# Layernorm passes moved into the head loop of a differential attention kernel, group by group

## What is computed

```
x = x + layernorm(differential_attention(layernorm(x)))   # 16 heads of 8
x = x + layernorm(windowed_transformer(layernorm(x)))     # two layers, rotary tables cos and sin
x = x + layernorm(state_space(layernorm(x)))
x = x + layernorm(mixture_of_experts(layernorm(x)))
```

```
m = mean(x); v = var(x)                    # per token, over 128 channels
y = (x - m) / sqrt(v + 1e-5)
q = q * qs * cos + rotate_half(q * qs) * sin    # so cos * qs and sin * (qs rotated) can be made once
```

## Time and profile before

| | us |
|---|---|
| median of 3 runs (lowest, highest) | 2048.75 (2048.04, 2049.25) |
| the profiled execution's own time | 2051.13 |
| its span, first to last instruction | 2049.3 |
| of it: head loop, first to last exponential | 37.1 to 737.5 |
| of it: end of the last sequence, to the last residual | 737.5 to 750.6 |
| of it: rotation tables | 750.9 to 752.6 |
| of it: layer norm of all groups | 753.3 to 768.7 |
| of it: windowed transformer and the rest | from 768.95 |

### The profile page before, as it was taken

One profiled execution on the slowest core, in us unless ns is written; L12 is line 12 of the kernel. 1 busy time (PEld: TensorE's weight loads), 2 busy tenths in 40 slices (PEclk: granted clock), 3 DMA queues, 4 the chain that ended last, 5 costly groups with the idle time before them and its releaser, 6 DMA issues. The chain is left out here.

```text
span 2049.3 us, 39274 instructions
## 1 busy us (share of the span) xinstructions
PE 1719.8 (84%) x12410; PEld 1128.4 (55%) x12410; DVE 1544.9 (75%) x4156; ACT 1363.4 (67%) x4708; POOL 877.9 (43%) x816
## 2 busy tenths in 40 slices
PE   4999999999999955999999695999999683753991
PEld 2555555555555532777777352777777351552660
DVE  2898889988889965899999365899998365663445
ACT  2888888888888862888888222888888226322555
POOL 3555655555655543233233123233233123285555
PEclk9999999999999976999999896999999896755995
DMA  7990000000000000000000100000000100012324
GB/s 205 185 184 11 2 1 2 1 2 1 2 2 2 2 1 6 12 17 12 16 17 12 32 19 6 11 17 13 16 16 13 32 19 1 6 45 66 84 64 133
DMA packets 102525, 65.90 MB, mean 32 GB/s; under 512 B 27698, under 2 KB 93874, under 8 KB 102322
## 3 DMA queue, kind: packets, MB, share of 16 engines
q1 hardware_dynamic: 97970, 54.40, 13.3%
q0 software_dynamic: 4352, 8.99, 1.3%
HBM read 19.50 MB, written 30.24 MB: 24 GB/s over the span
## 5 line engine op out<-in xcount | busy, mean ns | idle before, releaser
L411 ACT ACTIVATE a_E<-a_psS,a_nm 128x128 f32<-128x128 f32 (+1 forms) x1028 | 419.9, 429 | 32.2 <-DVE a_nm L245 30.2
L216 POOL TENSOR_SCALAR a_aT<-a_dT 128x384 f32<-128x384 f32 x256 | 309.1, 1208 | 299.8 <-PE a_psO L529 187.6
L245 DVE TENSOR_REDUCE a_nm<-a_psS 128x2 f32<-128x256 f32 (+1 forms) x514 | 259.9, 546 | 43.9 <-PE a_psS L496 43.4
L492 PE MATMUL a_psS<-a_kT,a_qm 32*128 32x128 f32 (+1 forms) x2064 | 240.6, 351 | 5.4 <-issue 3.4
L270 DVE SCALAR_TENSOR_TENSOR a_d<-a_E,a_cf 128x128 f32<-128x128 f32 (+1 forms) x512 | 219.4, 468 | 27.9 <-DVE a_cf L259 1.4
L411 ACT ACTIVATION_READ_ACCUMULATOR a_E<-a_psS,a_nm 128x1 f32 x1028 | 220.7, 215 | 0.0
L830 POOL TENSOR_TENSOR b0rn<-b0ss,minus_half 128x16 f32<-128x16 f32 x36 | 107.2, 2977 | 223.6 <-DVE b0ss L866 223.6
L830 POOL TENSOR_TENSOR b1rn<-b1ss,minus_half 128x16 f32<-128x16 f32 x36 | 107.2, 2977 | 223.0 <-DVE b1ss L866 223.0
L420 ACT ACTIVATE a_dT<-a_psT 128x384 f32<-128x384 f32 x256 | 127.0, 496 | 73.9 <-PE a_psT L505 71.2
L492 PEld LDWEIGHTS a_psS<-a_kT,a_qm 32*128 32x128 f32 x2064 | 136.6, 186 | 55.9 <-issue 35.6
L505 PE MATMUL a_psT<-ident,a_d 128*128 128x128 f32 x768 | 132.6, 282 | 6.8 <-DVE a_d L270 1.0
(11 more groups left out here) (353 smaller groups left out, 4424.1 us busy)
## 6 DMA issues: line engine op xcount, KB each, us to landing
mx_rows<-mx_blank SPq DMA_DIRECT2D x9, 2080.0 KB, 31.2
mx_xin<-mx_rows SPq DMA_DIRECT2D x72, 65.0 KB
b0v<-b0v SPq DMA_DIRECT2D x34, 128.0 KB, 2.3
b1v<-b1v SPq DMA_DIRECT2D x34, 128.0 KB
F<-mx_results SPq DMA_DIRECT2D x8, 256.0 KB, 5.2
mx_second<-mx_results SPq DMA_DIRECT2D x8, 256.0 KB, 5.4
out_dram<-X SPq DMA_DIRECT2D x8, 256.0 KB, 2.3
f0z<-F SPq DMA_DIRECT2D x9, 128.0 KB
```

What stands on the lines that cost most here:

```text
L216: pool.tensor_scalar(aT[:, s, :], dT[:, s, :], 0.0, None, ALU.max).then_inc(positived.sem, 1)
L245: ins = dve.tensor_reduce(nm[:, s, t, :], psS[:, s, :, (0, P)[t]:(P, 384)[t]], axis=AX.X, op=ALU.max, negate=True)
L411: ins = act.activation(E[:, s, m, c0:c1], psS[:, s, m, c0:c1], ACT.Exp, bias=nm[:, s, t, m:m + 1], accum_out=Z[:, p, h, t, m:m + 1])
L492: pe.matmul(psS[:, s, m, c0:c1], qm[rows, p, a, r, t * P:(t + 1) * P], kT[rows, p, a, 0:c1 - c0], start=(t == 0), stop=False)
```

## The change

1. `differential_attention` creates the `Layernorms` object of the sum at its start and does the work of the seam itself. `normalise_all` is gone.
2. For groups 0 to 6, in the second half of pair g+1: DVE takes the statistics of two tiles behind the mixing of step 8, of the other two behind that of step 9, and aggregates them (four instructions and the addition of 1e-5) behind step 15.
3. For groups 0 to 5, in the first half of pair g+2: POOL takes the power ahead of `positive` of head 1; DVE computes the shift behind step 1; ACT writes one tile to `F` ahead of its exponentials in each of steps 2, 3, 4 and 6.
4. Behind the loop: DVE scales the rotation tables, takes the shift of group 6 and half the statistics of group 7 before it finishes the last sequence, and the rest of group 7 after it. POOL takes the power of group 6 ahead of, and of group 7 behind, that of the last output. ACT writes the four tiles of group 6 behind its last `move_ot` and those of group 7 at the very end.
5. `hand_on` and one empty block follow (an additional barrier), then `window_attention`.

```diff
@@ -232,8 +234,12 @@
                         if h >= 12:
                             mask_heads(half + 1, 2 * (h - 12), 2 * (h - 11))
+                        if half == 0 and h == 1 and pair >= 2:
+                            ln.power(pool, pair - 2)
                         positive(pair, half, h)
+            ln.power(pool, LAST - 2)
             rstd(1, LAST, 0, 1)
+            ln.power(pool, LAST - 1)
@@ -382,8 +388,22 @@
                         if s == 14:
                             residual(pair, half)
+                        if half == 0 and s == 1 and pair >= 2:
+                            ln.shifts(dve, pair - 2)
+                        if half == 1 and pair >= 1:
+                            if s == 8:
+                                dve.wait_ge(added.sem, added.at(pair, 0, 1))
+                                ln.tile_statistics(dve, pair - 1, 0)
+                            if s == 9:
+                                ln.tile_statistics(dve, pair - 1, QT)
+                            if s == 15:
+                                ln.aggregate(dve, pair - 1)
                     own.end()
 
+            scale_tables(dve)
+            ln.shifts(dve, LAST - 2)
+            dve.wait_ge(added.sem, added.at(LAST - 1, 1, 1))
+            ln.tile_statistics(dve, LAST - 1, 0)
             own.begin(dve, LAST, 0)
@@ -395,6 +415,10 @@
             residual(LAST, 0)
+            dve.wait_ge(added.sem, added.at(LAST, 0, 1))
+            ln.tile_statistics(dve, LAST - 1, QT)
+            ln.aggregate(dve, LAST - 1)
+            ln.shifts(dve, LAST - 1)
@@ -467,6 +491,8 @@
+                        if half == 0 and s in (2, 3, 4, 6) and pair >= 2:
+                            ln.apply_tile(act, pair - 2, ln.tiles(F, pair - 2), (2, 3, 4, 6).index(s))
                         exps(pair, half + (s + 1) // H, (s + 1) % H)
@@ -474,9 +500,11 @@
             move_ot(LAST, -1, H // GH - 1)
+            ln.apply(act, LAST - 2, ln.tiles(F, LAST - 2))
             copy(OnT[:, :], psM[:, 0:T], misc_full.at(LAST, 0, E_ONT + 1))
             act.wait_ge(added.sem, added.at(LAST, 0, 0))
             copy(y[:, :, :], psM[:, T:512].rearrange("p (t n) -> p t n", t=QT), misc_full.at(LAST, 0, E_Y + 1))
+            ln.apply(act, LAST - 1, ln.tiles(F, LAST - 1))
@@ -2178,20 +2196,19 @@
-        differential_attention(nc, X, consts, wA, load_later)
+        differential_attention(nc, X, F, consts, wA, load_later, scale_tables)
         hand_on(nc)
+        with nc.Block():
+            pass
 
         if stop != "A":
-            with nc.Block() as block:
-                @block.vector
-                def _(dve):
-
-                    dve.wait_ge(loaded_later, 16 * len(later))
-                    for w in wB:
-                        for tab, s in (("cos", "scale"), ("sin", "scaler")):
-                            for t in range(QT):
-                                dve.tensor_tensor(w[tab][:, t], w[tab][:, t], w[s][:, :, :], ALU.mult)
-            normalise_all(nc, "n0", X, F, minus_half)
```

More of the change, by code:

```diff
@@ L101, with differential_attention @@
 CHAIN_M, CHAIN_M_PRE = 13, 10
-def differential_attention(nc, X, consts, weights, load_later):
+def differential_attention(nc, X, F, consts, weights, load_later, scale_tables):
     H, HD = 16, 8
@@ L177, in differential_attention @@
         own = Chain(sem("own"), CHAIN_A, 4)
+        ln = Layernorms(nc, ctx, "n0", X, minus_half)
         block = ctx.enter_context(nc.Block())
@@ L623, in statistics, with tile_statistics, aggregate @@
     def statistics(self, dve, g):
-        mv, src = self.mv[:, g], self.tiles(self.src, g)
-        for t in range(self.G):
+        for t in range(0, self.G, QT):
+            self.tile_statistics(dve, g, t)
+        self.aggregate(dve, g)
+    def tile_statistics(self, dve, g, first):
+        src = self.tiles(self.src, g)
+        for t in range(first, first + QT):
             ins = dve.bn_stats(self.st[:, t, :], src[:, t, :])
-        ins.then_inc(self.stats, 1)
+        if first + QT == self.G:
+            ins.then_inc(self.stats, 1)
+    def aggregate(self, dve, g):
+        mv = self.mv[:, g]
         dve.wait_ge(self.stats, g * 2 + 1)
@@ L642, in apply, with apply_tile @@
     def apply(self, act, g, dst):
-        act.wait_ge(self.shift_ready, g + 1)
-        src = self.tiles(self.src, g)
         for t in range(self.G):
-            ins = act.activation(dst[:, t, :], src[:, t, :], ACT.Identity, bias=self.shift[:, g, t:t + 1],
-                                 scale=self.rs[:, g, t:t + 1])
-        return ins
[L652 to L661, removed]
-        @block.vector
-        def _(dve):
[L665 to L674, removed]
+            ins = self.apply_tile(act, g, dst, t)
+        return ins
+    def apply_tile(self, act, g, dst, t):
+        if t == 0:
+            act.wait_ge(self.shift_ready, g + 1)
+        return act.activation(dst[:, t, :], self.tiles(self.src, g)[:, t, :], ACT.Identity,
+                              bias=self.shift[:, g, t:t + 1], scale=self.rs[:, g, t:t + 1])
 def add_normalised(nc, name, X, F, minus_half):
@@ L2179, in load_later, with scale_tables @@
                 sp.dma_start(region, mx["blank"][:, :].unsqueeze(1).broadcast_to([P, TILES, ROW])).then_inc(filled, 16)
-        differential_attention(nc, X, consts, wA, load_later)
+        def scale_tables(dve):
+            dve.wait_ge(loaded_later, 16 * len(later))
+            for w in wB:
+                for tab, s in (("cos", "scale"), ("sin", "scaler")):
+                    for t in range(QT):
+                        dve.tensor_tensor(w[tab][:, t], w[tab][:, t], w[s][:, :, :], ALU.mult)
+        differential_attention(nc, X, F, consts, wA, load_later, scale_tables)
         hand_on(nc)
+        with nc.Block():
+            pass
         if stop != "A":
-            with nc.Block() as block:
-                @block.vector
-                def _(dve):
-                    dve.wait_ge(loaded_later, 16 * len(later))
-                    for w in wB:
-                        for tab, s in (("cos", "scale"), ("sin", "scaler")):
-                            for t in range(QT):
-                                dve.tensor_tensor(w[tab][:, t], w[tab][:, t], w[s][:, :, :], ALU.mult)
-            normalise_all(nc, "n0", X, F, minus_half)
             for l in range(2):
```

## The result

| | before | changed |
|---|---|---|
| median (lowest to highest) of 9 runs each, us | 2048.72 (2045.91 to 2050.27) | 2043.66 (2041.34 to 2046.97) |
| the profiled execution's own time | 2051.13 | 2044.06 |
| its span | 2049.3 | 2042.3 |

The ratio is 0.9976, 95% interval 0.9966 to 0.9986: 5.1 us faster, a little over the 0.2% that I called measurable. Forecast were 2045.3 us and a gain of 3.4.

A forecast was written before the change was run, and what follows sets the result against it. DVE (step 13 over the sequence border to step 9) and PE in between set the pace. -12.8 + 0 + 3.2 + 5.9 + 0.3 = -3.4 us gave 2045.3 us; range 2042.5 to 2050.7, 8 in 10 2039.0 to 2052.0.

The forecast's parts named there:

- Part 3: Aggregation behind step 15, on the DVE-paced stretch: costs 0.54 us for each of six groups, 3.2 us.
- Part 4: Shift behind step 1 waits for POOL's power: costs 0.99 us per group, six groups, 5.9 us, the largest loop charge.
- Part 1: Seam between last residual and windowed transformer: shrinks from 18.37 to 5.53 us, a gain of 12.8 us.
- Part 2: Statistics behind steps 8 and 9: 0.80 us fits DVE's 0.80 us wait at step 10, cost 14 x 0.
- Part 5: 24 tiles on ACT in steps 2, 3, 4 and 6: mostly covered by waits, 0.05 us per group, 0.3 us.
- the signs: What would show it: windowed transformer starting 3.4 us earlier, six DVE waits of about 1.2 us, no step 10 wait.
- rival 3: Statistics not covered, the 0.80 us step 10 wait reappears behind them: +5.6 us, 2050.9 us; chance 0.13.
- rival 2: ACT becomes pace-setter, tiles of steps 3, 4 and 6 cost 6.9 us instead of 0.3: 2051.9 us; chance 0.12.
- Rival 1: The loop hides the stall for POOL's power as well: -9.3 us, 2039.4 us; chance 0.15.
- Rival 4: PE's stalls of 1 us in the loop let the granted clock fall; no size, chance almost nothing.

The follow-up runs named there:

- aggregation at step 11: Against the changed kernel, a group's aggregation on DVE moved from behind step 15 to behind step 11 of the second half; 2042.41 us, ratio 0.9981.
- power at head 0: Against the changed kernel, POOL's power put ahead of the positive part of head 0 instead of head 1; 2035.11 us, ratio 0.9955.
- tiles behind the loop: Against the changed kernel, ACT's 24 tiles of groups 0 to 5 taken out of the loop and put behind it; 2049.4 us, ratio 1.0016.
- the tables alone: Against the kernel before, only the 8 table instructions moved behind the loop, an empty block in their place; 2048.15 us against 2045.53, ratio 1.0005.

## Why the prediction was right, point by point

The sign, the size and the places were right; the single terms were less right than their sum. Part 3 was 1.3 us too dear and Part 4 1.2 too cheap, and that the two misses cancel is luck.

| term | forecast, us | measured, us | from |
|---|---|---|---|
| Part 1, the seam | -12.8 | -13.4 | 18.37 to 4.98 |
| Part 2, statistics | 0 | about 0 | step 10 without a wait; steps 8 to 11 together 0 |
| Part 3, aggregation | 6 x 0.54 = 3.2 | 6 x 0.31 = 1.9 | aggregation at step 11 |
| Part 4, shift behind the power | 6 x 0.99 = 5.9 | 6 x 1.18 = 7.1 | power at head 0 |
| Part 5, 24 tiles | 0.3 | 6 x 0.06 = 0.4 | tiles behind the loop |
| sum | -3.4 | -4.0 | |

The sum of the measured terms is 1.1 us from the 5.1 of the medians. The profiles have three further differences that the change does not explain: the 0.8 that four sequences of before had more, and the 0.9 and 1.4 us above. The first two are why the first instruction of the windowed transformer comes 5.6 us earlier (763.32) and not the 3.4 named among the signs.

**Part 1** missed by 0.6. "Barrier, `hand_on`, empty block and barrier took 1.28 us at the later seam": here they took 763.32 - (760.80 + 1.65) = 0.87. The statistics to the first tile took 2.42 instead of 2.55.

**Part 2** was right in its 0, but not because "they fit exactly". The lock re-timed the mixing and the coefficient around the wait of step 10, the maxima there came 0.14 us late, and the wait of step 12 (0.81 to 0.18) took the rest, which the prediction had not counted on. The same work at steps 0 and 1 cost 0.24 us a sequence, 1.7 in all, so even there it is far from the 5.6 us of rival 3.

**Part 3** is where a step failed. "0.49 + 0.15 - 0.10 = 0.54 us" is what the border costs. The error was to count PE's 0.10 as the only thing that comes back. Part 4 had used the lock between DVE and POOL for a coefficient that moves out of POOL's way. In Part 3 the whole next step moves the same way, and it was not asked there. It gives 0.2 us back through the mixing of head 0, and the net 0.31 lies below the lower end that the prediction gave, 0.39.

**Part 4** named the right wait and was too small by a fifth. The wait itself is what the prediction's rows give: DVE is free 0.24 us ahead of 655.60, the power is done at 656.77 and the shift starts 0.03 later, 1.44 us against 1.42 measured (the "about 1.2 us" among the signs does not follow from them). The miss is the shift. It was counted at 0.15 us and takes 0.47, because the power's end releases DVE's shift and POOL's next positive part at once. So the maxima of head 3 come 1.57 us later than with the power at head 0 (5.45 against 3.88 us behind head 0's reciprocal in sequence 14), not 1.27. Of this the coefficient gave back 0.28 as forecast. Another 0.11 came back in steps 3 to 5, where "nothing returns the rest" stood. 1.18 stay.

**Part 5** was right, and the experiment separates it from rival 2, whose 6.9 us the change does not pay. Its mechanism is real one step further: a tile in step 7 costs 0.41 us.

**Rival 1** (no stall) and **rival 3** fell with the rows of the changed kernel. **Rival 4** did not occur in the change and is real: the argument "such a stall is 1 us in 87" compared the wrong thing. The share of the loop in which PE stands says nothing about one uninterrupted pause.

Open: why the profiles differ behind the seam, by 1.4 us between the two compared, and what gave back most of the gain of the tables alone.

## What to carry to other kernels

Moving work from a seam into a loop is paid where an in-order engine meets a wait, not by the busy time that is added: well placed, the 15 instructions that a pair gained cost 0.07 us together; one shift of 0.15 us behind a late power cost 1.2. Ask of each added instruction when its input is ready in the timeline and put it one head away from there; in this kernel one digit (`h == 1` to `h == 0`) was worth 7 us, more than the whole change. Ask also who waits for its engine at that step: a tile of 0.49 us was nearly free in step 2 and cost 0.41 in step 7. Since DVE and POOL share a lock, a delay here also re-timed what followed against POOL, so take each two-input instruction of the next steps, not only the moved one.

## What the runs showed of the hardware that I had not expected

**Behind a PE pause of 2.73 us the granted clock fell to half, but not each time.** It fell behind five pauses in six and stayed at 1.00 behind one of the same length. The Trainium skill (page "TensorE: Matmul & The Clock Gate", section "Part 1: The HAM clock gate (the "warmup" mystery)") calls the activity monitor free-running, so that the point of a change varies with where the work happens to lie. The spared sequence 6 agrees; no run here shows the monitor itself.

**PE starts at half speed in every kernel here, for a time that differs.** The last eight score products at 1.65 us and the first eight at 0.92, in the kernel before:

```profile
38.87 1.65 PE L492 MATMUL a_psS<-a_kT,a_qm 32*128 32x128 f32 x8 [0.74 <-ACT a_E L411]
...
44.64 0.92 PE L492 MATMUL a_psS<-a_kT,a_qm 32*128 32x128 f32 x8
```

and in the kernel with only the tables moved:

```profile
47.64 1.65 PE L493 MATMUL a_psS<-a_kT,a_qm 32*128 32x128 f32 x8
...
53.64 0.92 PE L493 MATMUL a_psS<-a_kT,a_qm 32*128 32x128 f32 x8
```

Sequence 0 takes 46.17 us in the first and 49.74 in the second; over all profiles it is either 45.5 to 46.5 or 49.6 to 49.9, and the change itself has been seen with both (45.49, and 49.75 when run again). The clock column reads 1.00 over this stretch in both traces (below, 45 to 53 us with the tables moved), but there it rests on no record. The traces' own lists of clock changes begin, at full clock, at 44.55 us in the kernel before and at 52.79 with the tables moved, each ahead of the first products of 0.92 us; over all profiles at 43.2 to 45.7 where sequence 0 is short and at 52.6 to 53.3 where it is long. Ahead of the first record the durations of equal products are the witness:

```profile
45.00:53.00 8.00, 8.00 (x40) 4.71 (x42) 4.99 (x15) 3.09 (x15) 2.34 (x2) 1.00 1.13 354
```

This is some 4 us, nearly what the change gains. The eleven runs of the change on the later chip lie in two clusters, six at 2040.4 to 2042.8 and five at 2046.6 to 2047.0, and the one profiled, with the long sequence 0, is of the upper. That the start makes the clusters is likely but not shown: the profile of the kernel before has the short sequence 0 and one of its longest times. The medians of the tables' experiment, 2048.15 and 2045.53, differ mainly by how many runs fell into which cluster; the lowest (2044.88 and 2044.84) and the highest (2051.08 and 2051.21) agree, so the clusters are not what hid 1.5 us.
